# Attention scores from two float32r parts, two heads in the array's row groups, and 36 exponentials per quad

## The reference

```python
q = (x @ Wq (+ bq)).reshape(B, T, 16, 16).transpose(0, 2, 1, 3)     # k and v likewise
logits = einsum('bhqd,bhkd->bhqk', q, k) / sqrt(16)
logits = where(causal, -inf, logits)                               # 1024 x 1024 for each head
attn = softmax(logits)
out = einsum('bhqk,bhkd->bhqd', attn, v)                           # then times Wo, plus x
```

## Time and profile before

| | |
|---|---|
| median of 3 runs | 3067.8 us (3062.64 to 3068.69) |
| the profiled execution | 3063.85 us |
| its span in the trace | 3062.1 us |
| TensorE busy, mean granted clock | 2521.5 us, 0.894 |
| VectorE, ScalarE, GpSimd busy | 1970.2, 1461.2, 1099.6 us |
| heads_phase, first scores to last exponential | 764 to 1220 us and 2264 to 2718 us |
| one quad in the middle of heads_phase | 26.7 us, 32 quads in all |

### The profile page before, as it was taken

How to read it: one execution, slowest core, us unless ns; L and a number is a source line. 1 busy time by engine, 2 the same in 40 slices (tenths; PEclk the granted TensorE clock), 3 DMA queues, 4 the chain that set the end, 5 groups by cost and what they waited for, 6 DMA issues and landing times. The chain is left out here.

```text
span 3062.1 us, 49504 instructions
## 1 busy us (share of the span) xinstructions
PE 2521.5 (82%) x15250; PEld 1633.5 (53%) x15250; DVE 1970.2 (64%) x5480; ACT 1461.2 (48%) x3374; POOL 1099.6 (36%) x1558
## 2 busy tenths in 40 slices
PE   7956995886999999669749948984659999975998
PEld 6746992554233333457649937763423333324776
DVE  6755885664888884468638846743358888823544
ACT  4423552332477787124325523433418877751433
POOL 5773444665122222237744456610022222210000
PEclk9987997898799999679879969997769999986999
DMA  4454554555555552535445543313264555434010
GB/s 138 162 145 134 180 178 133 172 179 133 68 81 79 78 79 40 156 119 186 138 128 180 180 163 94 110 49 113 76 103 60 84 81 81 68 95 153 21 35 28
DMA packets 259904, 342.96 MB, mean 112 GB/s; under 512 B 37265, under 2 KB 193474, under 8 KB 259650
## 3 DMA queue, kind: packets, MB, share of 16 engines
q1 hardware_dynamic: 219714, 230.69, 32.9%
q0 software_dynamic: 39936, 109.11, 10.5%
HBM read 188.94 MB, written 149.43 MB: 110 GB/s over the span
## 5 line engine op out<-in xcount | busy, mean ns | idle before, releaser
L928 DVE CUSTOM_DVE_ANT_0 attn_heads_masked_s<-attn_heads_s_ps,attn_heads_causal 128x768 bf16<-128x768 f32 (+7 forms) x1024 | 726.7, 755 | 159.2 <-PE attn_heads_s_ps L821 157.8
L900 ACT ACTIVATE attn_heads_probs<-attn_heads_st_ps 128x512 f32<-128x512 f32 (+3 forms) x1536 | 659.2, 495 | 255.7 <-PE attn_heads_st_ps L840 242.8
L821 PE MATMUL attn_heads_s_ps<-attn_heads_k_st,attn_heads_q_st 96*128 96x512 bf16 (+3 forms) x1536 | 402.6, 343 | 53.9 <-DMA attn_heads_k_st<-k_dram 39.9
L840 PE MATMUL attn_heads_st_ps<-attn_heads_q_st,attn_heads_k_st 99*128 99x512 bf16 (+3 forms) x1536 | 420.0, 331 | 3.3 <-ACT attn_heads_probs L900 2.0
L856 PE MATMUL attn_heads_o_ps<-attn_heads_probs,attn_v_sb 128*32 128x512 f32 (+3 forms) x3072 | 326.9, 498 | 0.9 <-ACT attn_heads_oT L889 0.5
L840 PEld LDWEIGHTS attn_heads_st_ps<-attn_heads_q_st,attn_heads_k_st 99*128 99x128 bf16 x1536 | 135.6, 97 | 349.1 <-ACT attn_heads_probs L900 266.9
L1397 POOL DMA_INDIRECT xs_dram<-moe_route_xn,rows_at x256 | 272.6, 1065 | 79.0 <-issue 76.4
L792 POOL TENSOR_SCALAR_AFFINE_SELECT attn_heads_probs<-attn_heads_probs 128x512 f32<-128x512 f32 x256 | 163.1, 637 | 363.8 <-ACT attn_heads_probs L900 363.4
L1892 POOL DMA_DIRECT2D ys_dram<-moe_expert_y_sb x288 | 158.0, 549 | 242.2 <-DVE moe_expert_y_sb L2010 242.0
L821 PEld LDWEIGHTS attn_heads_s_ps<-attn_heads_k_st,attn_heads_q_st 96*128 96x128 bf16 x1536 | 135.6, 99 | 170.8 <-DVE attn_heads_row_max L928 72.7
L1966 ACT ACTIVATE moe_expert_xT_hi<-moe_expert_xT_ps 128x256 fp32r<-128x256 f32 x288 | 110.9, 385 | 195.7 <-PE moe_expert_xT_ps L1910 195.0
(11 more groups left out here) (264 smaller groups left out, 6043.4 us busy)
## 6 DMA issues: line engine op xcount, KB each, us to landing
moe_expert_x_sb<-xs_dram SPq DMA_DIRECT2D x288, 128.0 KB, 2.1
ys_dram<-moe_expert_y_sb POOLq DMA_DIRECT2D x288, 128.0 KB, 2.1
attn_heads_q_st<-q_dram SPq DMA_DIRECT2D x192, 128.0 KB, 6.9
attn_heads_k_st<-k_dram SPq DMA_DIRECT2D x192, 128.0 KB, 7.3
o_dram<-attn_heads_oT SPq DMA_DIRECT2D x64, 256.0 KB, 2.1
moe_route_w_raw<-in_L_ffn_we_dram SPq DMA_DIRECT2D x96, 128.0 KB
q_dram<-attn_proj_parts SPq DMA_DIRECT2D x32, 384.0 KB, 3.1
k_dram<-attn_proj_parts SPq DMA_DIRECT2D x32, 384.0 KB, 4.5
```

Of the source, the lines that this page charges most:

```text
L821: last = pe.matmul(s_ps[:, at + a // TILE, 0:w], q_st[0:DEPTH, r, h, i * P:(i + 1) * P], k_st[0:DEPTH, r, h, a:a + w], start=True, stop=True)
L840: pe.matmul(st_ps[:, v % NB, 0:w], k_st[0:ROWS, n % R, h, j * P:(j + 1) * P], q_st[0:ROWS, n % R, h, first:first + w], start=True, stop=Tr ...
L900: act.activation(probs[:, G % NR, h, 0:w], st_ps[:, v % NB, 0:w], ACT.Exp, scale=scale)\
L928: dve.tensor_tensor_reduce(out=masked_s[:, use % 4, 0:w], in0=s_banks[:, at * TILE:at * TILE + w], in1=causal[:, SEQ - w:SEQ], scale=1.0, ...
```

## The change

Four things are changed, all in the two attentions.

1. q and k are split into two float32r parts and not into three bf16 parts. `second` and `third` are gone, and so is `rest`: VectorE's subtraction writes the last part. The parts lie in a ring of six blocks with a semaphore each. A stored block has 128 x 2 x 512 x 4 bytes = 512 KB, where it had 384 KB.

```diff
+        parts = sb("parts", [P, RP, PARTS, TILE], F32R)
...
                         sp.wait_ge(parts_ready, t * 4 + m + 1)
                         sp.dma_start(dram[t // 2, :, rows, (t % 2) * TILE:(t % 2 + 1) * TILE].rearrange("l r t -> r l t"),
-                                     parts[:, t % 2, m, :, :]).then_inc(qk_stored[t % 2], 16)
+                                     parts[:, (4 * t + m) % RP, :, :].bitcast(F32)).then_inc(qk_stored[(4 * t + m) % RP], 16)
...
                 def first(t, m):
                     act.wait_ge(qk_full, 4 * t + m + 1)
-                    if t >= 2:
-                        act.wait_ge(qk_stored[t % 2], 64 * (t // 2))
-                    copy_part(parts[:, t % 2, m, 0, :], m, qk_ps[:, m, :]).then_inc(first_ready, 1)
-
-                def second(t, m):
-                    act.wait_ge(rest_ready, 4 * t + m + 1)
-                    act.activation(parts[:, t % 2, m, 1, :], rest[:, m % 2, :], ACT.Copy).then_inc(second_ready, 1)
+                    u = 4 * t + m
+                    if u >= RP:
+                        act.wait_ge(qk_stored[u % RP], 16 * (u // RP))
+                    copy_part(parts[:, u % RP, 0, :], m, qk_ps[:, m, :]).then_inc(first_ready, 1)
...
-                    first(t, 0)
-                    first(t, 1)
-                    second(t, 0)
-                    first(t, 2)
-                    second(t, 1)
-                    first(t, 3)
-                    second(t, 2)
-                    second(t, 3)
+                    for m in range(4):
+                        first(t, m)
...
                 def take_first(t, m):
...
+                    u = 4 * t + m
+                    one = parts[:, u % RP, 0, :].bitcast(F32)
...
                     else:
-                        dve.tensor_tensor(rest[:, m % 2, :], qk_ps[:, m, :], one, ALU.subtract).then_inc(rest_ready, 1)
-
-                def third(t, m):
-                    dve.wait_ge(second_ready, 4 * t + m + 1)
-                    dve.tensor_tensor(parts[:, t % 2, m, 2, :], rest[:, m % 2, :], parts[:, t % 2, m, 1, :], ALU.subtract)\
-                       .then_inc(parts_ready, 1)
+                        dve.tensor_tensor(parts[:, u % RP, 1, :], qk_ps[:, m, :], one, ALU.subtract).then_inc(parts_ready, 1)
```

```diff
-        q_st = sb("q_st", [P, R, QUAD, SEQ], BF16)
-        k_st = sb("k_st", [P, R, QUAD, SEQ], BF16)
-        row_max = sb("row_max", [P, 2, UNITS])
+        q_st = sb("q_st", [P, R, PAIR, SEQ], F32R)
+        k_st = sb("k_st", [P, R, PAIR, SEQ], F32R)
+        row_max = sb("row_max", [P, 2, P])
+        turned = sb("turned", [UNITS, 2, PARTS, P], F32R)
...
+                    for at, (ql, kl) in enumerate(((0, 0), (1, 0), (0, 1))):
+                        for g in range(2):
+                            to = slice(g * GROUP + at * HD, g * GROUP + (at + 1) * HD)
+                            sp.dma_start(q_st[to, r, :, :].bitcast(F32), q_v[ql][g]).then_inc(stack_loaded[r], 16)
+                            sp.dma_start(k_st[to, r, :, :].bitcast(F32), k_v[kl][g]).then_inc(stack_loaded[r], 16)
...
                 def put_max(m):
-                    sp.wait_ge(s_free, turn_over(m))
-                    sp.dma_start(q_st[DEPTH:ROWS, m % R, :, :].rearrange("l h t -> l (h t)"),
-                                 turned[0:SPLIT * UNITS, m % 2, :]).then_inc(neg_loaded[m % 2], 16)
+                    sp.wait_ge(s_free, use_of_turn(m) + 1)
+                    for g in range(2):
+                        for l in range(PARTS):
+                            row = g * GROUP + DEPTH + l
+                            sp.dma_start(q_st[row:row + 1, m % R, :, :].rearrange("l h t -> l (h t)").bitcast(F32),
+                                         turned[g * PAIR * QT:(g + 1) * PAIR * QT, m % 2, l, :].bitcast(F32)).then_inc(neg_loaded[m % 2], 16)
...
+                sp.wait_ge(ones_ready, 1)
+                for g in range(2):
+                    for r in range(R):
+                        for h in range(PAIR):
+                            sp.dma_start(k_st[g * GROUP + DEPTH:g * GROUP + ROWS, r, h, :].bitcast(F32), minus_one[:, :]).then_inc(ones_loaded, 16)
...
                 def turn_max(m):
-                    at, _, over = TURN_AT[m]
-                    pe.wait_ge(parts_ready, m + 1)
-                    pe.wait_ge(s_free, over)
-                    pe.matmul(s_ps[0:SPLIT * UNITS, at, 0:P], max_parts[:, m % 2, :], identb[:, :],
-                              start=True, stop=True).then_inc(s_full, 1)
+                    pe.transpose(s_ps[:, use % SB, 0:P], row_max[:, m % 2, :], ident[:, :]).then_inc(s_full, 1)
...
+                def split_turn(m):
+
+                    use = use_of_turn(m)
+                    dve.wait_ge(s_full, use + 1)
...
+                    high = turned[:, m % 2, 0, :]
+                    dve.tensor_copy(high, s_ps[0:UNITS, use % SB, 0:P]).then_inc(high_ready, 1)
+                    dve.wait_ge(high_ready, m + 1)
+                    dve.tensor_tensor(turned[:, m % 2, 1, :], s_ps[0:UNITS, use % SB, 0:P], high.bitcast(F32), ALU.subtract).then_inc(s_free, 1)
```

```diff
+FILL_ORDER = ((0, 7), (1, 7), (0, 0, 6), (0, 4, 2), (1, 5, 1), (None, 3), (1, 4, 2), (1, 0, 6), (0, 1, 5))
+HEAD_ORDER = (2, 0, 3, 1)
+LEAD = 14
+PACE = (4, 4, 5, 6, 7, 8, 12, 12, 12, 12, 13, 16, 16, 16, 19, 19, 21, 23, 26, 26, 27, 28, 30, 31, 33, 34, 36, 36, 38,
+        38, 40, 42, 42, 45, 47, 48)
+TURN_AFTER = 1
+COPY_AFTER = (6, 18)
+
+VALUES_AFTER = {2: -2, 5: -1, 9: 0, 12: 1, 15: 2, 21: 3, 24: 4, 26: 5, 31: 6, 35: 7}
...
-    UNIT_AT, TURN_AT = score_banks(NQ, SB)
+    SB, OB = 2, 1
...
+                    low = (h % 2) * GROUP
+                    made = pe.matmul(s_ps[:, use % SB, to:to + w], q_st[low:low + DEPTH, r, h // 2, i * P:(i + 1) * P],
+                                     k_st[low:low + DEPTH, r, h // 2, a:a + w], start=True, stop=True)
+                    if part == len(products) - 1:
+                        made.then_inc(s_full, 1)
+                        if f == TURN_AFTER and n > 0:
+                            turn_max(n - 1)
```

```diff
-STEPS = [(half, j) for half in range(2) for j in range((half + 1) * SUB)]
+STEPS = [(0, (0,)), (0, (1, 3)), (0, (2,)), (1, (0,)), (1, (1,)), (1, (2,)), (1, (3,)), (1, (4,)), (1, (5, 7)), (1, (6,))]
+    PIECE = []
+    for s in range(S):
+        share = TILE // step_width(s)
+        if share == 1:
+            PIECE += [(s, [h]) for h in HEAD_ORDER]
+        else:
+            PIECE += [(s, [g, g + 2]) for g in (HEAD_ORDER[0] % 2, 1 - HEAD_ORDER[0] % 2)]
+    PIECES = len(PIECE)
+    FIRST_PIECE = [[s for s, _ in PIECE].index(s) for s in range(S)] + [PIECES]
...
+                def scores_t(n, p):
+                    s, heads = PIECE[p]
+                    v = n * PIECES + p
                     if v >= NB:
                         pe.wait_ge(exp_done, v - NB + 1)
-                    pe.matmul(st_ps[:, v % NB, 0:w], k_st[0:ROWS, n % R, h, j * P:(j + 1) * P],
-                              q_st[0:ROWS, n % R, h, first:first + w], start=True, stop=True).then_inc(st_full, 1)
+                    low = (heads[0] % 2) * GROUP
+                    for x, h in enumerate(heads):
+                        for j, first, w, at in step_columns(s):
+                            to = x * step_width(s) + at
+                            last = pe.matmul(st_ps[:, v % NB, to:to + w], k_st[low:low + ROWS, n % R, h // 2, j * P:(j + 1) * P],
+                                             q_st[low:low + ROWS, n % R, h // 2, first:first + w], start=True, stop=True)
+                    last.then_inc(st_full, 1)
...
+                        if len(heads) == 1:
+                            to, from_ = probs[:, G % NR, heads[0], 0:w], st_ps[:, v % NB, 0:w]
+                        else:
+                            to = probs[:, G % NR, heads[0]:heads[1] + 1:heads[1] - heads[0], 0:w]
+                            from_ = st_ps[:, v % NB, :].rearrange("p (h t) -> p h t", t=w)
+                        act.activation(to, from_, ACT.Exp, scale=scale).then_inc(exp_done, 1)
```

321 lines of the change are left out of this document (147 added, 174 removed).

## The result

The changed kernel takes 3099.8 us (median of 4 runs, 3094.0 to 3101.6) where the kernel before took 3065.2 us in the same comparison (3060.8 to 3068.7): 1.011 times as long, with a 95% interval of 1.009 to 1.0131. It is 1% slower; the forecast was 2980 us. The profiled execution has a span of 3097.7 us, 35.6 more than before (3062.1). Worked out from TensorE's first and last record of each stage: the two heads_phases take 475.2 and 478.4 us where they took 457.1 and 455.1 (+41.4), the first projection 249.9 for 245.2, the second 153.9 for 162.5, and everything else together 1740.2 for 1742.2.

The account below looks back on a forecast made before the run. TensorE's list was taken as the bound, 26.7 us a quad. Quads of 24.4 save 69 us, last quads 4, projections 15: 3063.9 - 69 - 4 - 15 = 2976, median 4 above, 2980 us; range 2920 to 3035.

Parts of the forecast that it names:

- The sum: Whole kernel: 69 us less in 30 quads, 4 in the last quads, 15 in the projections; execution 2976 us.
- TensorE in a quad (the walk): heads_phase: product list with two row groups side by side takes 21.4 us a quad, 21.9 with 0.5 on top.
- The waits: heads_phase quad: 1.4 us for copies out and masks, 0.7 for buffers and stops, 0.4 for the turned maxima.
- the two buffers: heads_phase: two 1024-column buffers replace singly freed banks; with stops of blocks with v, 0.7 us a quad added.
- late maxima: Rival, heads_phase: maxima late or buffers too few, TensorE stands about 1.3 us more; 25.7 us a quad, 3019 us, chance 0.22.
- VectorE's waits fall under 1.5 us: Sign of being right, heads_phase: VectorE's waits for TensorE go from 3.8 to under 1.5 us a quad.
- The clock: Rival, heads_phase: TensorE's gaps lower its clock to the 1.2 GHz level, walk over 35 us a quad; chance 0.02.
- ScalarE: heads_phase: 36 wide exponentials and two copies take 20.4 us a quad, from 21.41 busy; 1152 exponentials of 512 columns.
- The turning: Quad's end: maxima path needs 5.5 to 6.9 us where 5.8 are available; 0.4 us a quad taken.
- The projections: Both projections: second 9 us less over 7 tiles, first 8 less (0 to 11), stores 2 more; 15 us together.
- One file: Rival, heads_phase: row groups don't run side by side; 28.1 us a quad, 3095 us, chance 0.12.
- two buffers too few: Rival, heads_phase: TensorE stands at each fill, about 1.3 us more a quad; 3019 us, chance 0.22 shared with late maxima.

Follow-up runs that it names:

- e14: Changed kernel with exponentials cut to half their columns and reductions to at most 512 columns: 3127 us (3211 before), 24.2 us a quad at full clock.
- e9: Changed kernel with all products in one row group, but over nearly all rows (114 and 128): 3336 us (3206 before).
- e10: Changed kernel with the turned maxima sent in two DMAs, not four: 1.0075 of the kernel before.
- e4: Changed kernel with each VectorE reduction cut to at most 512 columns: 3013 us (3061 before).
- e17: Changed kernel with maxima and ones moved to rows 62 and 63 of each half, rows 48 to 61 zeroed; repeat run: 3054.2 us, 0.9978 of the kernel before.
- e18: The changed kernel once more, unaltered, beside the one with rows of zeros: 3095.6 us, 1.0106 of the kernel before.

## Why the prediction was wrong, point by point

*The sum.* The forecast execution was 2976 us, the profiled one 3099.4: 123 us. The 30 quads took 36 us more where 69 less were forecast: 105 us. The first projection took 4.7 us more where 8 less were forecast, 13. The last quads took 2.6 us more and not 4 less, 7; the starts 2. Against that, 4 us lie in the other stages and in what I had put down for the stores.

*TensorE in a quad (the walk): failed.* That two files exist was right, and so far the trace bears out the Trainium skill (TensorE: Matmul & The Clock Gate, Part 3). What I took from it was a file each at full rate: 21.4 us, and 21.9 with a little on top. With light VectorE and ScalarE 24.2 were measured. By the starts of TensorE's records in those quads (893.71 to 1015.28 us of e14) the blocks with v take 9.3 us and the turning 0.3, as forecast (9.2 and 0.4). The products of scores, with the entries into the blocks with v, take 14.8 us where the sum had 10.8 and 1.0: this term failed. It had the spacing of one file, 0.23 us, for each file all the time. Behind each stop the second pair comes after 0.34 us and not 0.23; there are 11 such stretches in a quad, so 1.2 us. This is no price of pairing: one file in e9 pays it too, and the bf16 of before doesn't. Another 1.4 us lie in the one stretch of the quad in which TensorE still waits for VectorE. The rest lies in pairs that come 0.24 to 0.29 us apart. The walk had no term for the weights, whose loads take 0.20 us where bf16 took 0.10; that they are the reason fits the starts but was not tried apart. At full clock a quad took 26.1 us for the 24.4 of the forecast, over 30 quads 51 of the 105 us.

*The waits: size near, by luck.* I added 2.5 us to the walk: 1.4 for copies out and masks, 0.7 for the two buffers, 0.4 for the turning. Lightening VectorE gives back 1.9 (26.1 less 24.2), and the stretch with the stop that is left holds up to 1.4 more. So nearly all of it is VectorE's pace with the two buffers, which I had at 0.7; the waits for copies out and masks are down to 0.2 us a quad, and late maxima cost nothing (e10). The forecast that VectorE's waits fall under 1.5 us was wrong: 4.6.

*The clock: failed, and by its reason.* I gave it 0.02, "because gaps stay below a microsecond". Short gaps alone don't bring it down, and it falls without any. The list of products in one row group has none and runs at 0.50; the kernel before with 8% of its time in gaps runs at 1.00; one file of full rows runs at 1.00. The change halves the rows of each product (96 and 99 to 48 and 50) and makes up for it only while two overlap. With so few rows the gaps do count: the same products with half the standing still (e4) keep the clock at 0.98, and with rows of zeros it is up in spite of the gaps. I had the rival's outcome with a part of its reason, and not the part that makes this kernel differ from the one before. I had the row counts before me, in the earlier trace rows and in the diff, and never asked what they do to the clock. The Trainium skill (TensorE: Matmul & The Clock Gate, Part 1) speaks of a monitor of how busy the engine is; I read that as gaps, and these runs show that the engine can be busy all the time and still be given the lower level. What it cost: the 30 quads take 836.9 us, with rows of zeros 785.1, 52 of the 105 us (from one profile of each; the first quads, which vary from run to run, are in it).

*ScalarE: right* in number and size: 1152 exponentials of 512 columns, ScalarE busy for 19.9 us a quad (20.4 forecast).

*The turning: harmless.* The four issues take 2.4 us, near my upper price of 3.0, and in some quads a weight load waits for their DMA, but e10 shows that a quad takes as long without that wait.

*The projections: the second right* (8.6 for 9), *the first wrong.* There GpSimd's gathers set the pace, the bound of zero that I had named: from the first gather's start to the last one's they take 232 us before and 237 after, and 232 again in e17 with the same projection as after, so the 4.7 us more are no effect of the change that I can show. Over the profiles of kernels with this projection, where the kernel before takes 3060 us, the stage takes 243 to 253 us.

*The rivals.* One file gave 3095 us, within 5 us of the measurement, and is false: pairs start together. A time that fits proves no mechanism. Late maxima cost nothing; two buffers too few is what VectorE's share comes to. The clock was the rival that came true, in part: from the second quad to the fifteenth it was at the lower level for 18% of the time (136 of 769 us), not for all of it.

## What to carry to other kernels

Splitting the array into row groups gives back time only if the products meet; and before the sum, compare rows times products at work before and after, because fewer rows at work can take TensorE's clock from 2.4 to 1.2 GHz with the engine never standing still, and make short stops count that cost nothing before. Rows that a product doesn't need may be filled with zeros: here that cost nothing and was worth 1.3%. If a forecast rests on two things that run side by side, find or make a row that shows the spacing of the pair, not of its halves, and try a neighbouring order, since two products of lead made 18%.

## What the runs showed of the hardware that I had not expected

- TensorE's granted clock follows the rows that its products use: 0.50 with 48 and 50 rows in one file, busy 746.07 of 746.30 us; 1.00 with 114 and 128 rows in the same list; 1.00 with 96 and 99 rows in bf16 and 8% gaps. In the changed kernel, where pairs of 48 and 50 rows overlap for a part of the time, stops count as well: 0.89 with 4.7% of the time standing still (e18), 0.98 with 2.4% (e4).
- Rows of zeros beside rows of values count as rows at work: 0.89 to 0.99 and 1.00. Spare products made of zeros alone did not lift the clock ahead of the first quad: 0.50 over 47 us.
- Products of two row groups start within 0.01 us of each other, but pairs of 512 columns follow each other after 0.34 us behind a block with v and 0.23 to 0.29 later, where one file has 0.23. The 0.34 is there in one file of float32r too (e9), and not in bf16 (0.23).
- Weight loads of 128 columns take 0.20 us on the mean in float32r over 48 and 50 rows, and 0.10 in bf16 over 96 and 99.
- Four DMAs that write one row each take 2.4 us to issue, two that write two rows each 1.06.
